# Moving the side work of an attention and expert kernel to other steps, and a third tile in eight to ScalarE

## What is computed

```python
# x, ctx: (4, 512, 256); mask: (4, 1, 512, 512); adj: (512, 512)
q = heads(layernorm(x), Wq, bq); k = heads(ctx, Wk, bk); v = heads(ctx, Wv, bv)
scores = q @ k.T / sqrt(16) + adj
weights = softmax(where(mask == 0, -inf, scores))
x = x + tanh(g_xattn) * ((weights @ v) @ Wo.T + bo)
h = layernorm(x)
p = softmax(h @ gate_w.T)             # 8 experts
e = argmax(p)                          # one expert for each token
x = x + tanh(g_ffn) * p[e] * (relu(h @ w1[e] + b1[e]) @ w2[e] + b2[e])
```

## Time and profile before

| | before |
| --- | --- |
| median of 3 runs | 552.26 us (550.91 to 553.85) |
| the profiled execution's own time | 550.83 us |
| its span, first to last instruction | 549.1 us |
| PE busy | 524.0 us, 95% |
| PE weight loads busy | 408.5 us, 74% |
| DVE busy | 291.9 us, 53% |
| ACT busy | 313.3 us, 57% |
| POOL busy | 297.8 us, 54% |

### The profile page before, as it was taken

One profiled execution on the slowest core, in us unless ns is written; L12 is line 12 of the kernel. 1 busy time (PEld: TensorE's weight loads), 2 busy tenths in 40 slices (PEclk: granted clock), 3 DMA queues, 4 the chain that ended last, 5 costly groups with the idle time before them and its releaser, 6 DMA issues.

```text
span 549.1 us, 13316 instructions
## 1 busy us (share of the span) xinstructions
PE 524.0 (95%) x4099; PEld 408.5 (74%) x4148; DVE 291.9 (53%) x896; ACT 313.3 (57%) x687; POOL 297.8 (54%) x428
## 2 busy tenths in 40 slices
PE   8989999999999999999999998979999999999997
PEld 5577666667667667666676666658899999999996
DVE  2685577875667885567874678844340211111111
ACT  4366778666768676778676676664333333333332
POOL 6437566675467575468575456555144444444451
PEclk9999999999999999999999999989999999999999
DMA  8634615410405510204520058499137665555560
GB/s 293 194 112 136 193 48 193 145 41 1 154 21 179 178 50 1 79 10 150 189 79 3 10 159 276 137 354 335 60 102 217 212 204 192 180 184 188 191 208 2
DMA packets 51489, 77.68 MB, mean 141 GB/s; under 512 B 9944, under 2 KB 34600, under 8 KB 51304
## 3 DMA queue, kind: packets, MB, share of 16 engines
q1 hardware_dynamic: 46600, 67.72, 37.1%
q0 software_dynamic: 4192, 8.73, 5.0%
q10 hardware_dynamic: 640, 0.52, 0.3%
HBM read 52.76 MB, written 8.35 MB: 111 GB/s over the span
## 4 chain that ended last, share of the span: by engine, by line
PE 52%; DVE 3%; issue 2%; SPq 1%; ACT 1%; POOL 1%; DMA 1%; DVEq 0%; POOLq 0%; ACTq 0%
PE bank L1152 12%; PE bank L1162 11%; PE bank L963 8%; PE bank L975 5%; PE bank L1066 3%; PE bank L1088 3%; PE bank L952 3%; DVE prob L1618 2%; PE bank L851 1%; PE bank L886 1%; PE bank L936 1%; DMA slots<-slot_d 1%; ACT pt L1264 1%; PE bank L913 1%; PE bank L1129 1%
## 5 line engine op out<-in xcount | busy, mean ns | idle before, releaser
L1618 DVE CUSTOM_DVE_ANT_0 prob<-bank,adjm 128x512 f32<-128x512 f32 x256 | 172.5, 689 | 79.9 <-issue 54.0
L1264 ACT ACTIVATE pt<-bank 128x512 f32<-128x512 f32 x256 | 152.0, 596 | 88.1 <-PE bank L963 82.6
L690 POOL TENSOR_SCALAR prob<-prob,negmax 128x512 f32<-128x512 f32 x190 | 131.5, 695 | 119.3 <-DVE negmax L1618 114.0
L963 PE MATMUL bank<-ident,prob 128*128 128x128 f32 x1024 | 155.9, 275 | 10.0 <-POOL prob L690 3.0
L963 PEld LDWEIGHTS bank<-ident,prob 128*128 128x128 f32 x1024 | 125.5, 142 | 41.1 <-issue 14.3
L1341 ACT ACTIVATE adjm<-bank,colsm 128x128 f32<-128x128 f32 x184 | 52.5, 368 | 103.9 <-PE bank L1152 83.9
L952 PE MATMUL bank<-w2s 128*128 128x512 bf16 x208 | 79.2, 381 | 5.3 <-DVE negmax L1618 4.4
L975 PE MATMUL bank<-pt,vals 128*32 128x256 f32 x1024 | 68.3, 385 | 1.0 <-ACT vals L1226 0.5
L1152 PEld LDWEIGHTS bank<-xT,pt 128*128 128x128 f32 x576 | 67.1, 192 | 0.9
L1152 PE MATMUL bank<-xT,pt 128*128 128x128 f32 x576 | 67.2, 275 | 0.0
L1162 PE MATMUL bank<-w2s,adjm 128*128 x288 | 65.1, 379 | 0.0
(11 more groups left out here) (210 smaller groups left out, 626.9 us busy)
## 6 DMA issues: line engine op xcount, KB each, us to landing
pt<-in_L_ffn_w SPq DMA_DIRECT2D x19, 1024.0 KB, 5.0
w2s<-parts SPq DMA_DIRECT2D x96, 128.0 KB, 2.6
w2s<-in_L_ffn_w SPq DMA_DIRECT2D x8, 1024.0 KB, 9.7
maski<-in_mask_Bx1xSxS_ik SPq DMA_DIRECT2D x4, 1024.0 KB, 5.6
w2s<-parts SPq DMA_DIRECT2D x56, 64.0 KB, 2.1
xres<-in_x SPq DMA_DIRECT2D x18, 128.0 KB, 2.1
x_d<-rows SPq DMA_DIRECT2D x18, 128.0 KB, 1.8
xn_d<-rows SPq DMA_DIRECT2D x18, 128.0 KB, 1.9
```

Of the source, the lines that this page charges most:

```text
L690: po.tensor_scalar(prob[:, m], prob[:, m], -1.0, negmax[:, m:m + 1], ALU.mult, ALU.add).then_inc(s_shpool, 1)
L963: mm = pe.transpose(tr_bank[n % NTB][:, c * P:(c + 1) * P], prob[:, n % TILES % NB, c * P:(c + 1) * P], ident[:])
L1264: act.activation(pt[:, g % 2, :, j, q2 * P:(q2 + 1) * P], tr_bank[c % NTB][:].rearrange("p (c q) -> p c q", c=QT), ACT.Exp).then_inc(s_cac ...
L1618: ve.tensor_tensor_reduce(out=prob[:, m % NB], in0=sc_bank[m % NS][:], in1=adjm[:, qt], scale=-1.0, scalar=BIG, op0=ALU.add, op1=ALU.min, ...
```

## The change

It gives other steps to the work beside the tiles, in the ordinary batches (`USES`, first of each pair of tables), in the last batch (`LAST_USES`, second of each pair) and in the head, where the projection of the query's first half now stands ahead of turning the context's second half, because `next q` 0 has step 19 and `next ctx` 1 has step 22. `ACT_SHIFTS` goes from (3, 6) to (1, 3, 6), so ACT shifts 24 tiles in a batch where it shifted 16. `LAST_ACT_SHIFTS` goes from (60, 63) to (57, 62); these two are tiles 1 and 6 of an eight, which ACT has anyway, so tiles 60 and 63 of the last batch go to POOL. In all POOL has 160 shifts (190 before) and ACT 96 (66 before).

```diff
--- before.py
+++ after.py
@@ -67,8 +67,8 @@
     LO = LP + QT
     LAG = LO + 1
     FIRST_ACT = (5, 3, 0, 0)
-    ACT_SHIFTS = (3, 6)
-    LAST_ACT_SHIFTS = (60, 63)
+    ACT_SHIFTS = (1, 3, 6)
+    LAST_ACT_SHIFTS = (57, 62)
 
     def shift_on_act(n, last):
 
@@ -100,18 +100,18 @@
     PRE = len(PRO)
     FIRST_NEXT = PRO.index("next x")
     NEXT = 8
-    TAIL_A = [(15, "heads", 0), (18, "heads", 1), (23, "turn", 0), (25, "turn", 1), (29, "out", 0),
+    TAIL_A = [(16, "heads", 0), (18, "heads", 1), (23, "turn", 0), (25, "turn", 1), (29, "out", 0),
               (33, "out", 1), (38, "normed", 0), (41, "normed", 1), (44, "gate", (0, 1)), (51, "rank", 0)]
     USES = sorted([(10, "values", 0), (11, "values", 1)] + TAIL_A
-                  + [(12, "next x", 0), (14, "next x", 1), (17, "next ctx", 0), (19, "next ctx", 1),
-                     (20, "next q", 0), (26, "next k", 0), (30, "next q", 1), (35, "next k", 1)]
-                  + [(45, "heads", 2), (46, "heads", 3), (50, "turn", 2), (52, "turn", 3), (53, "out", 2),
-                     (56, "out", 3), (61, "normed", 2), (63, "gate", (2,)), (65, "normed", 3),
+                  + [(12, "next x", 0), (14, "next x", 1), (17, "next ctx", 0), (22, "next ctx", 1),
+                     (19, "next q", 0), (26, "next k", 0), (30, "next q", 1), (35, "next k", 1)]
+                  + [(43, "heads", 2), (46, "heads", 3), (49, "turn", 2), (52, "turn", 3), (53, "out", 2),
+                     (55, "out", 3), (61, "normed", 2), (66, "gate", (2,)), (65, "normed", 3),
                      (68, "gate", (3,))], key=lambda use: use[0])
-    LAST_USES = sorted([(10, "values", 0), (11, "values", 1), (13, "heads", 0), (14, "heads", 1), (16, "turn", 0),
-                        (18, "turn", 1), (20, "out", 0), (22, "out", 1), (27, "normed", 0), (29, "normed", 1),
-                        (31, "gate", (0, 1)), (39, "rank", 0), (45, "heads", 2), (46, "heads", 3), (48, "turn", 2),
-                        (50, "turn", 3), (52, "out", 2), (55, "out", 3), (60, "normed", 2), (62, "gate", (2,)),
+    LAST_USES = sorted([(10, "values", 0), (11, "values", 1), (13, "heads", 0), (14, "heads", 1), (17, "turn", 0),
+                        (18, "turn", 1), (20, "out", 0), (22, "out", 1), (28, "normed", 0), (29, "normed", 1),
+                        (32, "gate", (0, 1)), (39, "rank", 0), (45, "heads", 2), (46, "heads", 3), (48, "turn", 2),
+                        (50, "turn", 3), (52, "out", 2), (55, "out", 3), (57, "normed", 2), (64, "gate", (2,)),
                         (65, "normed", 3), (67, "gate", (3,))], key=lambda use: use[0])
     LAST_TAIL = [("heads", 0), ("heads", 1), ("rank", 0), ("turn", 0), ("turn", 1), ("out", 0), ("out", 1),
                  ("normed", 0), ("normed", 1), ("gate", (0, 1)), ("rank", 1)]
@@ -122,21 +122,21 @@
 
     ACT_AT, VE_AT, ACT_QK_AT, VE_QK_AT = 1, 1, 2, 3
     OUT_STATS_AT = VE_AT + 1
-    OUT_RSTD = ({32: 0, 36: 1, 56: 2, 59: 3}, {23: 0, 25: 1, 55: 2, 59: 3})
-    ROW_STEPS = ({36: 0, 39: 1, 59: 2, 63: 3}, {25: 0, 27: 1, 57: 2, 61: 3})
-    SHIFT_STEP, EXP_STEP, PICK_STEPS = (45, 33), (46, 34), ((47, 48, 49), (35, 36, 37))
-    STATS_STEPS, RSTD_STEP, NORM_STEPS = (61, 62, 64, 65), 67, (69, 70, 72, 73)
+    OUT_RSTD = ({32: 0, 38: 1, 54: 2, 59: 3}, {23: 0, 25: 1, 55: 2, 59: 3})
+    ROW_STEPS = ({36: 0, 39: 1, 58: 2, 63: 3}, {25: 0, 28: 1, 56: 2, 60: 3})
+    SHIFT_STEP, EXP_STEP, PICK_STEPS = (45, 33), (46, 34), ((47, 48, 52), (35, 36, 39))
+    STATS_STEPS, RSTD_STEP, NORM_STEPS = (61, 63, 64, 65), 65, (69, 68, 72, 73)
     CAST_STEPS = {n + VE_QK_AT + 1: (i, w, a) for i, (n, w, a) in enumerate(USES)
                   if w in ("next q", "next k")}
     SPLIT_STEPS = {n + 1: use for n, use in CAST_STEPS.items()}
-    SLOT_STEPS, SCATTERED_STEP = ((54, 59, 62, 67), (41, 43, 46, 47)), (73, 60)
-    TABLE_STEPS = (41, 42, 43, 44, 45, 48, 49, 50, 51, 52, 65, 66)
+    SLOT_STEPS, SCATTERED_STEP = ((52, 60, 62, 68), (42, 43, 48, 44)), (72, 61)
+    TABLE_STEPS = (41, 42, 43, 44, 47, 48, 49, 50, 51, 52, 64, 66)
     INDEX_STEP, NORMED_STEPS = TILES - 5, (TILES - 5, TILES - 2)
-    ABS_STEPS = {29: 0, 34: 1, 40: 2, 45: 3}
-    SHUT_STEPS = {31: 0, 36: 1, 44: 2, 48: 3}
-    FIRST_ABS_STEPS, FIRST_SHUT_STEPS = {1: 2, 4: 3}, {2: 2, 5: 3}
-    MASK_STEPS, LATE_MASK_STEPS = {42: 0, 44: 1}, {13: 2, 15: 3}
-    WV_STEP, BV_STEP, WO_STEP, BIAS_STEP, GATE_STEP, FIRST_NORM_STEPS = 3, 4, 6, 8, 9, (2, 3, 4, 5)
+    ABS_STEPS = {29: 0, 33: 1, 40: 2, 45: 3}
+    SHUT_STEPS = {31: 0, 37: 1, 47: 2, 46: 3}
+    FIRST_ABS_STEPS, FIRST_SHUT_STEPS = {1: 2, 5: 3}, {2: 2, 5: 3}
+    MASK_STEPS, LATE_MASK_STEPS = {42: 0, 44: 1}, {17: 2, 13: 3}
+    WV_STEP, BV_STEP, WO_STEP, BIAS_STEP, GATE_STEP, FIRST_NORM_STEPS = 3, 3, 3, 7, 8, (1, 3, 7, 6)
     assert min(USES)[0] >= LAG and max(USES)[0] + 3 < LAG + TILES
     PER = len(USES)
     LAST_SHIFT = len(LAST_USES) - PER
```

## The result

The changed kernel takes 545.55 us in the median of 4 runs (544.84 to 546.48), the kernel before 551.59 beside them (4 runs); the ratio is 0.9893 with a 95% interval of 0.9845 to 0.9942. Five later runs of the changed kernel beside 17 of the kernel before on another chip gave 0.9894 (0.9871 to 0.9916). The profiled execution took 544.84 us, its span is 543.1 us where it was 549.1.

A forecast was written before the change was run, and what follows sets the result against it. It took PE to set the pace, so only PE's short waits could be won. The terms -3.3 - 0.6 + 1.2 + 0.7 - 0.4 gave -2.4 us, a forecast of 549.9 us, range 546.3 to 553.3 (8 in 10).

The forecast's parts named there:

- A: VectorE, tiles 46 to 50: heads 2 and route_weight leave the row of masks 47 to 50; 1.1 us a batch, -3.3 us.
- B: Batch boundary: a norm statistic goes behind mask 63, shortening waits in batches 0 and 1; 0.3 us each, -0.6 us.
- C: Third shift on ScalarE: delays an exp at tile 57 and, in the last batch, tile 25; 0.3 us each, +1.2 us.
- D: End of batch 3: GpSimd's longer queue behind the slot lists delays the weighings, at the low clock; +0.7 us.
- E: Head: the query's first half goes first, so SP's copies start earlier; gain uncertain behind the key part's subtract; -0.4 us.
- rival on the head's clock: Head: PE's filler ends early, PE idles about a microsecond and the clock halves; +1.8 us, 551.7 us, chance 0.06.
- ScalarE's rival: ACT becomes the bound: added shifts hold an exp in all eight groups of three batches; +3.9 us, 556.2, chance 0.10.
- all of DVE's lag goes: Tile stretch: three quarters of PE's waits for DVE vanish and ACT has room; -5.9 us, 546.4 us, chance 0.22.

The follow-up runs named there:

- e1_window: Kernel before with only the ordinary batches' moves around masks 47 to 50 (heads 2, route_weight, turn 2, out 3 and their steps): 546.9 us, ratio 0.9932.
- e7_norms: Kernel before with only the norm's steps changed (second statistic 62 to 63, its rstd 67 to 65, first two norms to 69 and 68): 549.9 us, ratio 0.9969.
- e8_gate: Kernel before with only gate 2 moved from step 63 to 66 in batches 0 to 2: 551.4 us, ratio 1.0008.
- e3_two: Changed kernel with both shift tuples of before, (3, 6) and (60, 63), so all steps moved but no third shift: 543.8 us, ratio 0.9872.
- e14: Changed kernel with the last batch's tables and LAST_ACT_SHIFTS of before, as e4, run on the chip of e15: 549.45 us.
- e15: The changed kernel itself, run again on the chip of e14: 548.39 us.
- e4: Changed kernel with the last batch's tables and LAST_ACT_SHIFTS of before: 547.7 us, ratio 0.9942.
- e5: Kernel before with the last batch's new tables alone, not its shifts: 549.6 us, ratio 0.9979.
- e6: Kernel before with two last-batch numbers changed, normed 2 at step 57 for 60 and its row at 56 for 57: 549.95 us, ratio 0.9976.
- The fillers: Idle matmuls before tile 61 in the last batch: 18 or 20 in the kernel before (ratios 0.9987, 0.9983), 20 in e4's kernel (548.57 us).
- e2_third: Kernel before with ACT_SHIFTS (1, 3, 6) alone, tiles 60 and 63 kept on ScalarE: 553.8 us, ratio 1.005.

## Why the prediction was wrong

| step | forecast | measured | by |
| --- | --- | --- | --- |
| A, masks 47 to 50 | -3.3 (0 to -5.8) | -4.1 | e1_window, milestones (-3.7 by its ratio) |
| B, boundary | -0.6 (0 to -1.6) | -1.6 | e7_norms and e8_gate |
| C, third shift | +1.2 (+0.5 to +18.9) | +1.2 | changed kernel against e3_two, up to `base_i` |
| D, end of batch 3 | +0.7 (+0.1 to +1.5) | -1.1 | e14 against e15, uncertain by 1.7; e4's ratio against e15's -2.6; e5 and e6, without GpSimd's longer queue, -1.2 |
| E, head | -0.4 (-0.9 to +1.0) | 0.0 | nine profiles of either head |

The measured column sums to -5.6, the whole change is -5.9, and 0.3 more lie between tiles 8 and 32 of the batches. The agreement to 0.1 is luck: terms read from ratios are known to 1 or 2 us. The profiled pair differs by 6.0 us for partly other reasons: its lists came 1.0 us sooner by chance, and behind them nothing was won.

**D is the step that failed**, and the only one whose sign and bounds were wrong. It read the earlier trace rows rightly: the idle of 2.43 us, the stretch at the lower level of 1.2 GHz behind it, the lists of DMAs that set the time. It even placed normed 2 at step 57, waiting for its row, inside those 2.43 us. The error was the next sentence: it took the low clock as a fixed part of this place and asked only how much work would now lie in it. But the wait at step 57 doesn't hide in the idle, it takes it away from there: 1.61, 0.76, 0.23 and 0.41 us in four places instead of 2.43 in one. The clock then stayed at 2.4 GHz, in this profile and in all 34 executions with normed 2 at step 57 on chips with the short wait for `region`, where it had fallen in 44 of 61 of the kernel before, at 1.0 to 2.7 us each. The price that D did name, GpSimd's longer queue, was real: 1.1 us from `early_index` to tile 63's transposes, with +0.7 forecast. The last batch gained all the same because more than this was saved by the clock, and some tenths before `base_i`. The bounds, +0.1 to +1.5, left a gain out without a reason. The forecast's own rival on the head's clock says that a fall follows an idle, and it wasn't asked in D what takes that idle away. The Trainium skill, page "TensorE: Matmul & The Clock Gate", section "What's actually happening", says that the throttled state is the default and activity releases it; by that sentence a kernel with a shorter idle keeps the higher clock longer, which is what the runs show. The fillers agree: 0 falls in 3 profiles with them, 6 in 8 without.

**B's mechanism was right, its size too small.** "PE would wait there for part of it" was priced at half and more of the gain. The two waits behind the boundary (0.23 and 0.22) were there before too, so what was put behind mask 63 cost nothing new; and 0.72 us a boundary came back, nearly the 0.8 that the range had as its end. The idle of 0.50 that B read in the earlier trace rows was partly a missing record; 0.28 in a full trace. **A** took 1.1 of a possible 1.94 and got 1.36; that DVE at 82% would ask it back soon was too careful. Under the third shift the same stretch gains 1.1, so part of A's gain and C's price lie in the same steps.

**C was right in size and half right in place.** Beside the moved steps tile 57 costs 0.16 to 0.2 us and tile 25 of the last batch 0.2, where 0.3 was forecast for each. The waits of transposes for `pt` rose to 1.4 us in 3. The places not foreseen were tile 49 (0.23 us) and the start of batch 3 (0.3), so the right sum is partly luck. The point of ScalarE's rival, 0.14 us for each of 24 shifts, wasn't reached: 1.2 us over 30 shifts are 0.04. That it isn't free shows in e2_third at the old steps, 2.7 us by its ratio: the price of a shift depends on how late the masks in front of it are.

**E.** SyncE's copies started at 17.41 where it was 18.09, and the key part's subtract took 0.69 instead of 1.64; ScalarE's copies started at 21.02 all the same (21.09 in the earlier trace rows), because TensorE projected the context only at 16.34 after 1.30 us of idle. The rule of the shared ports was read too far: it says that the two instructions contend, and the forecast took it that the subtract is the one to wait. It did not: the subtract (20.30) began 0.17 us before GpSimd's mask (20.47, 1.66 us), and here it was the mask that was slow (the one before it, beside no subtract, took 1.27). In the kernel before the mask had begun first, at 18.98, 0.43 us ahead of the subtract.

```profile
20.30 0.69 DVE L1697 TENSOR_TENSOR parts<-rest,parts 128x512 bf16<-128x512 f32 x1
```

```profile
20.47 1.66 POOL L617 TENSOR_TENSOR adjm<-adjr,maski 128x512 f32<-128x512 f32 x1 [1.70 <-ACT maski L1253]
```

The Trainium skill, page "SBUF — State Buffer", section "Who interferes with whom", calls the shared ports an exclusive lock; the trace agrees in both kernels, with 1.64 us for the subtract in one and 1.66 for the mask in the other.

**The base.** The forecast stood on a median of 552.26 us from 3 runs, which with 4 runs was 551.59: 0.7 of the 4.35 us by which 549.9 was too high. D is 1.8 of them, A and B 1.8 together. The rival "all of DVE's lag goes" had nearly the right time, 546.4, with C at 0.5 and D at +0.4, so for a partly wrong reason; its B was right, though, and its A no farther off than the forecast's.

## What to carry to other kernels

Where the granted clock dips behind an idle, ask of each change whether it makes that idle shorter or longer before pricing any work that lies in the dip; a wait put ahead of an unavoidable one cost nothing here and kept the clock. One or two profiles can't tell how often a clock falls; the mean granted clock of every execution can. Work that only stands between an engine and what others wait for is worth moving even when it is a few tenths of a microsecond, and in the order of an in-order queue the price of an added piece depends on whether the piece in front is late. When a change bundles a load shift with step moves, time them apart: here the moves won 7 us and the new shift tuples took 1.2 to 1.4 of them back.

## What was unexpected of the hardware

- An idle of TensorE of 2.1 to 2.7 us was followed by a stretch at 1.2 GHz in 6 of 8 profiles of nearly the same code and not in the other 2, and by the mean clock in 84 of 114 executions, so one profile doesn't tell what such an idle costs: 0.9 to 2.7 us or nothing.
- The same program differs between chips in one wait (`region`, 0.3 or 1.6 to 2.0 us) and by 3 us in all (551.1 to 551.6 in three comparisons, 554.1 and 554.6 us in the two with the longer wait, for the kernel before), while the ratio of the changed kernel was the same, 0.9893 and 0.9894.
- A two-input VectorE instruction of 0.69 us took 1.64 behind a GpSimd one that had begun first, and 0.69 when it began 0.17 us ahead of it.
